# A sixteen-head perceiver attention on one core: how the reciprocals of the softmax sums reach the rows that they scale

## What is computed

```python
q, k, v = (split_heads(t) for t in (q, k, v))
q = q * scale
sim = jnp.einsum('bhid,bhjd->bhij', q, k)
sim = jnp.where(full_mask[:, None, None, :], sim, max_neg)
attn = jax.nn.softmax(sim, axis=-1)
out = jnp.einsum('bhij,bhjd->bhid', attn, v)
out = out.transpose(0, 2, 1, 3).reshape(b, m, INNER)
out = jnp.einsum('bne,ed->bnd', out, Wout)
return layer_norm(out, g_o, b_o)
```

## Time and profile before

| | us |
|---|---|
| median of 3 runs (2098.76 to 2102.35) | 2100.9 |
| the profiled execution | 2084.4 |
| its span, first to last instruction | 2082.6 |
| turns of the last attention, about 1102 to 1975 of the span | 873.0 |
| PE busy in these turns | 850.7 |
| DVE busy there | 769.9 |
| ACT busy there | 464.8 |

### The profile page before, as it was taken

One profiled execution on the slowest core, in us unless ns is written; L12 is line 12 of the kernel. 1 busy time (PEld: TensorE's weight loads), 2 busy tenths in 40 slices (PEclk: granted clock), 3 DMA queues, 4 the chain that ended last, 5 costly groups with the idle time before them and its releaser, 6 DMA issues.

```text
span 2082.6 us, 33216 instructions
## 1 busy us (share of the span) xinstructions
PE 1921.5 (92%) x11797; PEld 1355.2 (65%) x11797; DVE 1435.7 (69%) x2676; ACT 978.5 (47%) x2079; POOL 752.3 (36%) x1145
## 2 busy tenths in 40 slices
PE   6997799696999988997878999999999999998999
PEld 3885799542699976883565666666675666655644
DVE  5775111467344457787867999999878999998755
ACT  5672333343111252226875555555545555555455
POOL 1002111000522200000006777777656777777500
PEclk9897899898999999998989999999999999999999
DMA  3702899502489960002002333333222333333201
GB/s 115 208 2 79 273 323 333 170 1 86 163 292 321 310 228 1 1 1 86 1 13 60 82 83 82 83 83 83 72 57 72 82 82 82 82 82 81 63 1 41
DMA packets 191184, 226.87 MB, mean 109 GB/s; under 512 B 28939, under 2 KB 167085, under 8 KB 191021
## 3 DMA queue, kind: packets, MB, share of 16 engines
q1 hardware_dynamic: 183725, 201.98, 33.0%
q0 software_dynamic: 7296, 22.78, 3.3%
HBM read 127.64 MB, written 29.91 MB: 76 GB/s over the span
## 4 chain that ended last, share of the span: by engine, by line
PE 45%; ACT 6%; DVE 3%; issue 1%; POOL 0%; ACTq 0%; DVEq 0%; POOLq 0%
PE ps L640 41%; ACT w_odd L1796 4%; PE ps L1214 2%; PE ps L1215 1%; ACT arena L1785 1%; PE ps L1106 0%; DVE w_odd L2532 0%; DVE small L2410 0%; POOL arena L1908 0%; ACT out_feat L1708 0%; PE ps L1115 0%; ACT xn_tok L1651 0%; DVE small L2522 0%; ACT out_feat L1714 0%; DVE arena L2380 0%
## 5 line engine op out<-in xcount | busy, mean ns | idle before, releaser
L1908 POOL COPY arena<-w_odd 32x512 f32<-32x512 f32 x1024 | 623.7, 609 | 254.4 <-DVE w_odd L2532 202.1
L640 PE MATMUL ps<-arena,w_odd 128*128 128x128 f32 (+4 forms) x2352 | 468.2, 441 | 3.0 <-DVE arena L2202 1.2
L640 PE MATMUL ps<-arena 128*64 128x256 f32 (+4 forms) x3248 | 392.3, 370 | 8.3 <-DVE arena L2333 4.4
L640 PEld LDWEIGHTS ps<-arena 128*64 128x64 f32 (+4 forms) x3248 | 258.9, 155 | 119.5 <-issue 22.6
L2532 DVE STREAM_TRANSPOSE w_odd<-w_odd 128x1024 f32<-128x1024 f32 x256 | 317.4, 1245 | 14.6 <-ACT w_odd L1796 3.0
L1796 ACT ACTIVATE w_odd<-ps,small 128x1101 f32<-128x1101 f32 x256 | 301.6, 1179 | 48.0 <-DVE small L2522 41.0
L640 PEld LDWEIGHTS ps<-arena,w_odd 128*128 128x128 f32 (+3 forms) x2352 | 286.3, 188 | 27.9 <-issue 18.7
L1781 ACT ACTIVATE arena<-ps 77x256 f32<-77x256 f32 x128 | 48.5, 379 | 295.4 <-PE ps L1215 295.4
L2522 DVE TENSOR_REDUCE small<-ps 128x1 f32<-128x1101 f32 x128 | 166.9, 1304 | 29.3 <-PE ps L640 28.1
L1893 POOL DMA_INDIRECT token_rows<-arena x62 | 59.8, 964 | 292.3 <-DVE arena L2223 292.3
L2523 DVE TENSOR_REDUCE small<-ps 128x1 f32<-128x1024 f32 x128 | 155.4, 1214 | 0.0
(11 more groups left out here) (398 smaller groups left out, 2909.8 us busy)
## 6 DMA issues: line engine op xcount, KB each, us to landing
arena<-w_odd SPq DMA_DIRECT2D x1024, 64.0 KB
w_odd<-in_s_w SPq DMA_DIRECT2D x32, 1024.0 KB, 7.4
w_odd<-in_s_wgu SPq DMA_DIRECT2D x30, 704.0 KB, 6.1
w_even<-in_s_w SPq DMA_DIRECT2D x15, 1024.0 KB, 7.3
arena<-expert_rows_in SPq DMA_DIRECT2D x62, 130.0 KB, 4.7
w_odd<-in_s_wd SPq DMA_DIRECT2D x30, 256.0 KB, 3.6
out_feat<-in_s_wgu SPq DMA_DIRECT2D x10, 704.0 KB, 5.9
expert_rows_in<-zero_row POOLq DMA_DIRECT2D x1, 5070.0 KB, 33.2
```

Source lines behind the costliest of these rows:

```text
L640: return pe.matmul(o, lhsT, rhs, start=start, stop=stop, **kw)
L1908: pool.tensor_copy(s6_d[u % 4][32 * j:32 * j + 32, :, 256 * i:256 * i + 256], s6_pm[u % 2][32 * i:32 * i + 32, :, 256 * j:256 * j + 256]). ...
```

## The change

The reciprocals take another way. In even turn u ACT's queue writes the 128 x 4 reciprocals of group (u-2)/2 to a small array in device memory, so that each unit and head has a row of 128 there. In odd turn u ACT's queue reads them back by two transfers, one for each head, each of which gives 64 partitions the same two rows of 128. They land in `s6_r`, where DVE reads them as before. `sums_turn`, its key "r" and the copy at L1785 are gone; DVE waits for the two reads (`rows_in`) where it waited for the copy, and its reciprocal waits for the write of two groups ago (`rows_out`) where it waited for the product. The array has two slots.

```diff
+        rows_dram = nc.dram_tensor("sum_rows", [2, 2, 2, P], F32).ap()
+        rows_out, rows_in = sem("rows_out"), sem("rows_in")
...
-            if even and 2 <= u < NU + 2:
-                batch += [("r", (u - 2) // 2)]
...
-                def sums_turn(g):
-
-                    pe.wait_ge(a6_rb, g + 1)
-                    bank = free_bank(("r", g))
-                    for i in range(2):
-                        for h in range(2):
-                            r = 64 * h
-                            last = mm(PS[r:r + 64, bank, i * P:(i + 1) * P], s6_rc[:, g % 2, 2 * i + h:2 * i + h + 1].broadcast_to([P, DH]), ident[:, :])
-                    last.then_inc(r6_mm, 1)
...
-                    if even and 2 <= u < NU + 2:
-                        sums_turn((u - 2) // 2)
...
+                    if even and 2 <= u < NU + 2:
+                        g = (u - 2) // 2
+                        act.wait_ge(a6_rb, g + 1)
+                        if g >= 2:
+                            act.wait_ge(rows_in, 32 * (g - 1))
+                        act.dma_start(rows_dram[g % 2].rearrange("i h q -> q (i h)"), s6_rc[:, g % 2], allow_slow_non_contiguous=True).then_inc(rows_out, 16)
+                    if not even and 3 <= u < NU + 3:
+                        g = (u - 3) // 2
+                        act.wait_ge(rows_out, 16 * (g + 1))
+                        if g >= 2:
+                            copied(act, ("v", g - 2))
+                        for h in range(2):
+                            act.dma_start(s6_r[g % 2][64 * h:64 * h + 64].rearrange("p (i q) -> p i q", i=2),
+                                          rows_dram[g % 2][:, h].partition_broadcast(64)).then_inc(rows_in, 16)
...
-                    if even and 2 <= u < NU + 2:
-                        g = (u - 2) // 2
-                        bank = filled(("r", g))
-                        act.activation(s6_r[g % 2], PS[:, bank, 0:2 * P], ACT.Copy).then_inc(r6_act, 1)
...
-                        copied(dve, ("r", g))
+                        dve.wait_ge(rows_in, 32 * (g + 1))
...
-                                dve.wait_ge(r6_mm, r6_no["r", g - 2] + 1)
+                            if g >= 2:
+                                dve.wait_ge(rows_out, 16 * (g - 1))
```

More of the change, by code:

```diff
@@ L394, in build @@
             for key in batch:
-                eng = "act" if key[0] in "crwn" else "dve"
+                eng = "act" if key[0] in "cwn" else "dve"
                 done[eng] += 1
```

## The result

The changed kernel takes 2226.0 us (median of 4, 2223.7 to 2231.3) where the kernel before takes 2101.6 beside it: a ratio of 1.060, 95% interval 1.059 to 1.062. The prediction was 2095.4, faster.

The account below looks back on a forecast made before the run. PE's work and the softmax loop were taken to bound turns, none ordinary under 6.24 us. Gains of 6.9 less 1 for SP hold-ups and 0.4 for the clock gave -5.5: 2100.9 to 2095.4 us, 8-in-10 range 2091 to 2118.

Parts of the forecast that it names:

- The write as one issue: ACT's write in even turns: lands after 4 us (bounds 2.0 and 5.3), may hold SP 0.6 late; 1 us loss taken.
- a room: Odd unit's last SP transfer lands at 1171.7, `weigh` starts at 1173.11: 1.4 us to spare.
- The write holds up SP: Rival: 60 odd turns lose what a hold-up of SP exceeds 1.4 us; 2113 to 2131; chance 0.23 for +5 and more.
- The gains: PE without `sums_turn`: 3.1 us from 26 even turns, 3.6 from projection turns, 0.2 at most elsewhere; 6.9 us in all.
- the projection turns: Turns 60, 62, 64, 66, 124 and 126, long and on PE, keep all 0.6 us each, 3.6 us.
- The copy on ACT: Dropping ACT's copy of 0.38 us, 64 times, gains 0, since it and the maximum end almost together.
- all 38.4 are kept: Rival: all of PE's 38.4 us are gained, 2062; needs a softmax loop under 6.24 us; chance 0.01.
- The reads: ACT's two reads for odd turns: 1.2 us of issue, 2.5 to land, there at 1175.0, wanted at 1178.0; hidden.
- no change: Rival: contention and clock take as much as the projections give, 2098 to 2103; within 0.2% had chance 0.34.
- ACT behind the table load: Rival: reads start after ACT's table load, adding 1.2 us in six turns after projections; 2105; 0.31 together with small losses.
- The clock: PE's drops to 1.2 GHz after idle time, as at turn 120: 1 to 2 us either way, 0.4 taken as loss.

Follow-up runs that it names:

- e4: Changed kernel with the write cut into 128 pieces of 16 bytes instead of 512 of 4; 2087.7 us, 1.001 of the kernel before.
- e6: e1 with the same 512 pieces of 4 bytes written into SBUF instead of device memory; 2086.7 us, 1.000 of the kernel before.
- e1: Changed kernel with the write kept, but both reads fetch rows of ones and wait for no write; 2260.4 us, 1.084 of the kernel before.
- e3: Changed kernel with no write and no reads, the multiply's rows set to one once; 2081.2 us, 0.997 of the kernel before.
- e2: Changed kernel without the write, its two reads fetching rows of ones; 2089.5 us, 1.001 of the kernel before.
- e9: Kernel before plus the element-wise write, issued some 4.9 us into the even turn, nothing read back; 2308.6 us, 1.106 of the kernel before.
- e13: Kernel before plus the element-wise write, issued 1.4 us into the odd turn, nothing read back; 2228.8 us, 1.064 of the kernel before.
- e14: Kernel before plus two element-wise writes in a row, the second to its own array, nothing read back; 2273.5 us, 1.083 of the kernel before.
- e8: Changed kernel with a write of 16-byte pieces and reads in 2 KB rows, DVE taking every second number; 2098.1 us, 1.006 of the kernel before.
- e16: e15 with one read for both heads instead of two; 2253.1 us, 1.073 of the kernel before.
- e15: e8 with the reads issued 1.4 us into the odd turn; 2096.3 us, 0.999 of the kernel before.

## Why the prediction was wrong

**The write as one issue: the step that failed.** The prediction bounded the write's landing by 2.0 and 5.3 and took 4; it is 8.3, outside. It bounded what the write does to SP by one issue of 0.6 to 1.99, and put +1 us for it in its sum, since "the bytes have room, only a shared way of issuing could do it". Bytes were the wrong unit. The issue cost ACT 0.37, and SP's median issue stays at 0.597 (longest 4.1 instead of 2.0). The landing of the transfers moved, by 3.4 at the median and 5.3 at most, against a room that was rightly read as 1.4. In the place of the +1 the changed kernel has 92.8 us of PE idle before `weigh` and 34 of slower products. (64 times 2, the median excess over the room, is 128 and close to the loss of 124. That is partly luck, for it leaves out the clock: the idle time alone is 1.5 for each `weigh`, not 2.)

**The rival "The write holds up SP"** had the place, the victim (`weigh` in odd turns) and the sign right, and its price, 60 odd turns times the excess over 1.4, too. It had 0.23 of the chance and ended at 2131, since its longest hold-up was SP's longest issue. With the measured 3.4 to 5.3 the same formula gives 120 to 234 us, without a term for the clock. The Trainium skill's rule against a strided last dimension, in "DMA: Bandwidth & Descriptors", section "Rules for kernel authors", was cited and set aside because the page has no price. e4 against the changed kernel is that price here, 1.001 against 1.060. The same page, section "Why small descriptors are slow (HBM only)", restricts the penalty to device memory, and e6 agrees: its write lands in 2.3 us, that of e1 in 9.2.

**The gains.** Sized well: even turns 6.24, never 6.36; odd turns 6.55 where `weigh` is on time; the projection turns lost 0.78 each, not 0.6. Predicted 6.9; the floor e3 gives 5.7 (3.8 to 7.9), and in its profiled execution the even turns are 7.3 shorter and the odd ones 2.6 longer. The copy on ACT is worth nothing, as said. No turn of e3 or of the changed kernel fell under 6.23, so the rival "all 38.4 are kept" is void.

**The reads** were held to be hidden. Without the write's fault they cost 8 us (e2 less e3). In the profiled executions 5.3 of it lie in the gap behind the last turn, where nothing covers the last group's read, and 0.1 in the turns; the prediction looked only at turns. Even without the write's fault the change would have come out level (e4: 0.7 us over before, which is "no change").

**ACT behind the table load.** Void: e4 issues reads while ACT computes, as rows above show, and its turns 61, 63, 65 and 67 last 6.55, 6.68, 6.59 and 6.59 as before. The Trainium skill, "Perfetto Trace Analysis", section "Per-engine timelines", has compute instructions wait in a queue while the sequencer decodes on; for transfers the trace agrees (reads at 1194.75, and the copies that stand before them in the code from 1195.50). But an issue that waits stops this, as 1216.73 in the changed kernel shows, and it made ACT's copy 3.4 late in the turn shown. PE was later still: nothing of it lies on the path there, as the 4.2 us of idle before the scores in question tell (5.5 before).

**The clock.** Taken as 0.4; it is 34. Of the 42 waits before `weigh`, 19 (1.6 to 4.1 us, median 3.8) are followed by products at the lower clock, which take 1.3 to 3.0 longer together; 5 waits of 1.5 to 2.3 are not. The prediction knew the effect from turn 120 and looked for it only at the place of the old pause.

## What to carry to other kernels

Price a transfer by its pieces and where they land, not by its bytes alone: here 512 pieces of 4 bytes into device memory took 8.3 us and delayed another queue's transfers, 128 pieces of 16 bytes took 1.6, and into SBUF 512 took 2.3. Bound an unseen transfer by a row of its own kind or leave the upper end open; the nearest row of another kind is no bound. If rows go through device memory, place the transfers between the landing that others wait for and the next instruction of the issuing engine, and give the last pass, which nothing covers, the short way.

## What was not expected of the hardware

- Small pieces into device memory land in 1.6, 3.2 and 8.3 us as pieces of 16, 8 and 4 bytes (2 KB in all), and with pieces of 4 bytes 2% of SP's packets of 1 KB then take over 1 us (551 of 23723), most of them 5 to 7 us after the issue. Why is open: no run separates the size of the pieces from their number, or from their lying side by side in the array. Open too is the rule by which a transfer behind such a write waits: e9, e13 and e14 show that its place moves the loss between 123 and 222 us and that two writes cost 1.4 times one.
- The multiply with a stride of 16 bytes in its second operand takes 0.586 us (e8) instead of 0.424 in the changed kernel and 0.390 before.
- A read whose slowest dimension is 2 had two late landing events instead of sixteen, and landed in 8.5 us instead of 3.8 (e16, e15).
